# One PSUM bank moved from the side work to the exponentials, and the causal masks of the maxima added by TensorE: a causal attention in a four-block network

## The reference

```python
x = x + 0.5 * moe(layernorm(x));  x = x + attn0(layernorm(x));  x = x + 0.5 * moe(layernorm(x))
x = x + 0.5 * fp4(layernorm(x));  x = x + attn1(layernorm(x));  x = x + 0.5 * fp4(layernorm(x))

def attn0(x, Wqkv, Wout, bout):          # x: 4 sequences x 1024 tokens x 128; 16 heads of 8
    q, k, v = split_heads(x @ Wqkv.T)
    dots = einsum('bhid,bhjd->bhij', q, k) * 8 ** -0.5
    dots = where(key later than query, -inf, dots)
    return merge_heads(einsum('bhij,bhjd->bhid', softmax(dots), v)) @ Wout.T + bout
```

## Time and profile before

| | |
|---|---|
| median of 3 runs | 1891.05 us (1888.12 to 1892.08) |
| profiled execution, its own time | 1890.3 us |
| its span, first to last instruction | 1888.3 us |
| first exponential unit of the first attention | at 358.2 us |
| first exponential unit of its last round | at 870.1 us |
| mean granted TensorE clock | 0.929 |

### The profile page before, as it was taken

How to read it: one execution, slowest core, us unless ns; L and a number is a source line. 1 busy time by engine, 2 the same in 40 slices (tenths; PEclk the granted TensorE clock), 3 DMA queues, 4 the chain that set the end, 5 groups by cost and what they waited for, 6 DMA issues and landing times. The chain is left out here.

```text
span 1888.3 us, 35242 instructions
## 1 busy us (share of the span) xinstructions
PE 1582.2 (84%) x12162; PEld 1091.1 (58%) x12167; DVE 1220.6 (65%) x2516; ACT 1056.5 (56%) x2103; POOL 693.1 (37%) x1145
## 2 busy tenths in 40 slices
PE   6997975899999999999799799346788888988774
PEld 5666863555555555553666577234566766667653
DVE  6633558887887888883664366465656777766544
ACT  2433432488888888887243244213566667667651
POOL 0786552111111111111058665352234545544342
PEclk9998997899999999999699899767899999999987
DMA  6122322011111111110413123200000000000000
GB/s 246 38 78 66 109 68 70 23 40 29 27 36 29 34 29 28 40 29 12 183 45 88 59 82 101 102 1 1 2 2 2 5 5 8 5 8 8 7 4 12
DMA packets 50494, 83.08 MB, mean 44 GB/s; under 512 B 11124, under 2 KB 35124, under 8 KB 49652
## 3 DMA queue, kind: packets, MB, share of 16 engines
q1 hardware_dynamic: 41236, 62.07, 11.4%
q0 software_dynamic: 9088, 18.76, 2.9%
HBM read 43.18 MB, written 31.22 MB: 39 GB/s over the span
## 5 line engine op out<-in xcount | busy, mean ns | idle before, releaser
L1920 DVE TENSOR_REDUCE z_parts<-z_pM 128x4 f32<-128x512 f32 x576 | 373.0, 685 | 95.9 <-PE z_pM L1658 92.1
L1835 ACT ACTIVATE z_Pr<-z_pE 128x512 f32<-128x512 f32 x576 | 322.2, 596 | 86.7 <-PE z_pE L1682 83.9
L1682 PE MATMUL z_pE<-z_QM,z_QK 128*128 128x512 f32 x576 | 251.0, 438 | 8.9 <-DMA z_QM<-z_Q 6.6
L2027 POOL TENSOR_SCALAR_AFFINE_SELECT z_Pr<-z_Pr 128x512 f32<-128x512 f32 x128 | 81.3, 635 | 481.2 <-ACT z_Pr L1835 481.2
L1658 PE MATMUL z_pM<-z_KM,z_Q 128*128 128x512 f32 x576 | 233.4, 410 | 1.5 <-DVE z_Q L1910 0.9
L1682 PEld LDWEIGHTS z_pE<-z_QM,z_QK 128*128 128x128 f32 x576 | 108.1, 188 | 159.3 <-ACT z_Pr L1835 91.5
L356 POOL DMA_INDIRECT slot_results<-m_yq,m_xq x156 | 153.7, 985 | 108.5 <-ACT m_yq L561 79.9
L332 POOL DMA_INDIRECT slot_rows<-m_XN,m_dest x128 | 129.3, 1010 | 94.5 <-DVE m_dest L650 59.2
L1695 PE MATMUL z_pO<-z_Pr,z_V 128*9 128x512 f32 (+3 forms) x1536 | 159.3, 488 | 0.1
L974 PE MATMUL f_gup<-s_wguT,f_xT 128*128 128x352 f32 x234 | 102.6, 523 | 33.8 <-DVE f_src L1281 18.9
L1658 PEld LDWEIGHTS z_pM<-z_KM,z_Q 128*128 128x128 f32 x576 | 109.4, 191 | 18.4 <-DVE z_parts L1920 3.2
(11 more groups left out here) (290 smaller groups left out, 3870.3 us busy)
## 6 DMA issues: line engine op xcount, KB each, us to landing
slot_rows<-in_c_pad SPq DMA_DIRECT2D x2, 5070.0 KB, 24.6
m_xq<-slot_rows SPq DMA_DIRECT2D x38, 260.0 KB
z_QM<-z_Q SPq DMA_DIRECT2D x128, 64.0 KB, 2.0
z_KM<-z_QK SPq DMA_DIRECT2D x60, 128.0 KB, 2.4
m_raw<-in_gu SPq DMA_DIRECT2D x2, 2048.0 KB, 8.7
m_XN<-slot_results SPq DMA_DIRECT2D x8, 512.0 KB
m_raw<-slot_results SPq DMA_DIRECT2D x8, 512.0 KB, 5.6
slot_results<-m_yq,m_xq POOLq DMA_INDIRECT x156
```

What stands on the lines that cost most here:

```text
L1682: mm(pE[e % 2][:, :].rearrange("p (h c) -> p h c", h=4), QK[G % RING][:, kt * P:(kt + 1) * P], QM[half][:, :, q * P:(q + 1) * P], start=Tr ...
L1835: a.activation(Pr[j % 4][:, :, q * P:(q + 1) * P], pE[e % 2][:, :].rearrange("p (h c) -> p h c", h=4), ACT.Exp, scale=DH0 ** -0.5).then_in ...
L1920: v.tensor_reduce(parts[:, qt, kb, :], pM[n % 3][:, :].rearrange("p (h k) -> p h k", h=4), AX.X, ALU.max).then_inc(maxed, 1)
L2027: g_.affine_select(blk, blk, [[0, 4], [1, P]], ALU.is_ge, 0.0, base=0, channel_multiplier=-1).then_inc(selected, 1)
```

## The change

The side work gives one of its two banks to the exponentials. `pE` becomes three banks, and an exponential unit waits for unit e - 3 to be done instead of e - 2. All side work goes through the one bank `pX`, and the waits of each step are put on the last reader of the step before. The slots of the side work are set anew, and the order of the projections becomes first half of queries, first half of keys, second half of keys, second half of queries. The transfer of the keys waits for three projections of its round instead of two. ScalarE's mask writes and their semaphore go; every diagonal maximum unit is followed by the bf16 matmul that round 0 had.

```diff
-        pE = [s.ps(f"pE{u}", [P, 512]) for u in range(2)]
+        pE = [s.ps(f"pE{u}", [P, 512]) for u in range(3)]
-        pX, pO = [s.ps(f"pX{u}", [P, 512]) for u in range(2)], s.ps("pO", [P, 512])
+        pX, pO = s.ps("pX", [P, 512]), s.ps("pO", [P, 512])
...
-        AT_M1, AT_O1, AT_FIN, AT_K, AT_O0, AT_Q, AT_M0 = 4, 10, (13, 14), (16, 18), 21, (23, 29), 27
+        AT_M1, AT_O1, AT_FIN, AT_O0, AT_M0 = 4, 11, (14, 16), 22, 29
+        Q_LOW, K_LOW, K_HIGH, Q_HIGH = 2, 0, 1, 3
+        AT_PROJECT = (7, 18, 25, 31)
+        ORDER = (Q_LOW, K_LOW, K_HIGH, Q_HIGH)
...
-                        sp.wait_ge(split_done, 4 * (G + 2) + 2)
+                        sp.wait_ge(split_done, 4 * (G + 2) + 3)
                         sp.wait_ge(sm_ready, NM * (G + 1))
                         spread_keys(G + 2, slice(0, SEQ0), k_masked[G % 2])
...
-                    if G and kb == qt:
-                        pe.wait_ge(filled, len(DIAG) * (G - 1) + DIAG.index(n) + 1)
                     last = mm(pM[n % 3][:, :].rearrange("p (h k) -> p h k", h=4), Q[G % 2][:, qt * P:(qt + 1) * P],
-                              KM[G % 2][:, :, kb * P:(kb + 1) * P], start=(G == 0 or kb < qt), stop=(G > 0 or kb < qt), skip_group_check=True)
-                    if G == 0 and kb == qt:
+                              KM[G % 2][:, :, kb * P:(kb + 1) * P], start=True, stop=(kb < qt), skip_group_check=True)
+                    if kb == qt:
                         last = mm(pM[n % 3][:, :], identb[:, :], after_query[:, :], start=False, stop=True, skip_group_check=True)
...
-                    need(pe, exp_done, NE * G + e - 1)
-                    mm(pE[e % 2][:, :].rearrange("p (h c) -> p h c", h=4), QK[G % RING][:, kt * P:(kt + 1) * P],
+                    need(pe, exp_done, NE * G + e - 2)
+                    mm(pE[e % 3][:, :].rearrange("p (h c) -> p h c", h=4), QK[G % RING][:, kt * P:(kt + 1) * P],
...
                         if e == AT_M1:
+                            need(pe, split_done, min(4 * (G + 2), 4 * NG))
                             need(pe, m_kept, 2 * G + 1)
                             turn_maximum(G, 1)
+                        if e == AT_PROJECT[0] and further:
+                            need(pe, m_kept, 2 * G + 2)
+                            project(G + 2, Q_LOW)
                         if e == AT_O1 and G > 0:
-                            need(pe, split_done, min(4 * (G + 2), 4 * NG))
+                            need(pe, *((split_done, 4 * (G + 2) + 1) if further else (m_kept, 2 * G + 2)))
                             turn_output(G - 1, 1)
                         if e in AT_FIN and first:
-                            need(pe, m_kept, 2 * G + 2)
+                            need(pe, o_normed, 2 * G)
+                            need(pe, fin_kept, 2 * (G // 4 - 1) + AT_FIN.index(e))
                             turn_batch(G // 4 - 1, AT_FIN.index(e))
-                        if e in AT_K and further:
...
+                        if e == AT_PROJECT[1] and further:
+                            need(pe, split_done, 4 * (G + 2) + 1)
+                            need(pe, o_normed, 2 * G)
                             if first:
...
+                                need(pe, fin_kept, 2 * (G // 4))
+                            project(G + 2, K_LOW)
                         if e == AT_O0:
...
+                            if further:
+                                need(pe, split_done, 4 * (G + 2) + 2)
+                            else:
+                                need(pe, o_normed, 2 * G)
                             turn_output(G, 0)
-                        if e in AT_Q and further:
...
+                        if e == AT_PROJECT[2] and further:
+                            need(pe, o_normed, 2 * G + 1)
+                            project(G + 2, K_HIGH)
                         if e == AT_M0 and more:
-                            need(pe, o_normed, 2 * G + 1)
+                            if further:
+                                need(pe, split_done, 4 * (G + 2) + 3)
+                            else:
+                                need(pe, o_normed, 2 * G + 1)
                             turn_maximum(G + 1, 0)
+                        if e == AT_PROJECT[3] and further:
+                            need(pe, m_kept, 2 * G + 3)
+                            project(G + 2, Q_HIGH)
...
-                def fill_mask(G, n):
...
-                    act.wait_ge(maxed, NM * G + n - 2)
-                    a.activation(pM[n % 3][:, :], after_query[:, :], ACT.Copy).then_inc(filled, 1)
...
-                        if more and e + 2 in DIAG:
-                            fill_mask(G + 1, e + 2)
```

More of the change, by code:

```diff
@@ L1623, in project @@
                     for w, xx, a, b in ((wh, xh, True, False), (wh, xl, False, False), (wl, xh, False, True)):
-                        last = mm(pX[BANK[i]][:, :], w[:, c:c + P], xx[:, xs], start=a, stop=b)
+                        last = mm(bank(G, i)[:, :], w[:, c:c + P], xx[:, xs], start=a, stop=b)
                     last.then_inc(proj_done, 1)
@@ L1667, in turn_maximum @@
                     c = slice(half * 512, half * 512 + 512)
-                    mm(pX[0][:, :], identr[:, :], Q[G % 2][:, c], start=True, stop=False, skip_group_check=True)
+                    mm(pX[:, :], identr[:, :], Q[G % 2][:, c], start=True, stop=False, skip_group_check=True)
                     for j in range(4):
-                        last = mm(pX[0][:, j * P:(j + 1) * P], mw[:, 4 * half + j, :, :].rearrange("p h c -> p (h c)"), identr[:, :],
+                        last = mm(pX[:, j * P:(j + 1) * P], mw[:, 4 * half + j, :, :].rearrange("p h c -> p (h c)"), identr[:, :],
                                   start=False, stop=(j == 3), skip_group_check=True)
@@ L1701, in turn_output @@
                     for j in range(4):
-                        last = nc.tensor.transpose(pX[half][:, j * P:(j + 1) * P], oT[:, j * P:(j + 1) * P], ident[:, :])
+                        last = nc.tensor.transpose(pX[:, j * P:(j + 1) * P], oT[:, j * P:(j + 1) * P], ident[:, :])
                     last.then_inc(o_turned, 1)
@@ L1707, in turn_batch @@
                     for j in range(4):
-                        last = nc.tensor.transpose(pX[half][:, j * P:(j + 1) * P], at[:, half * 4 + j, :], ident[:, :])
+                        last = nc.tensor.transpose(pX[:, j * P:(j + 1) * P], at[:, half * 4 + j, :], ident[:, :])
                     last.then_inc(fin_turned, 1)
@@ L1910, in split @@
                     v.scalar_tensor_tensor(dst[:, (i % 2) * 512:(i % 2) * 512 + 512], high[:, :].bitcast(F32),
-                                           rows[:, 3 - i // 2:4 - i // 2], pX[BANK[i]][:, :], ALU.mult, ALU.add).then_inc(split_done, 1)
+                                           rows[:, 3 - i // 2:4 - i // 2], bank(G, i)[:, :], ALU.mult, ALU.add).then_inc(split_done, 1)
                 def max_unit(G, n):
@@ L1953, in main @@
                             output(G - 1, 1)
-                        for i in range(2):
-                            if n == AT_K[i] + LATE and further:
-                                split(G + 2, i, i)
+                        for k in range(4):
+                            if n == AT_PROJECT[k] + LATE and further:
+                                split(G + 2, ORDER[k], k)
                         if n == AT_O0 + 2:
                             output(G, 0)
-                        for i in range(2):
-                            if n == AT_Q[i] + LATE and further:
-                                split(G + 2, 2 + i, 2 + i)
                         if n < NM and more:
```

37 lines of the change are left out of this document (13 added, 24 removed).

## The result

The kernel after takes 1920.5 us (median of 4 runs, 1916.9 to 1924.67), beside 1889.59 for the kernel before: a ratio of 1.0168, 95% interval 1.0142 to 1.0194, some 31 us slower. The forecast of 1930 was right in direction and in order of size, 8 us too high in the loss. The profiled execution took 1916.9 with a span of 1915.0.

What follows compares the result with a forecast made beforehand. In full rounds TensorE was taken as a stream without holes except one 0.35 us wait. Terms 27.8 + 13.7 + 5.2 + 2.4 - 5.3 - 1.9 - 3.1 = +38.8 us on 1891.05 gave 1930, range 1907 to 1943.

Steps and rivals of the forecast that it cites:

- C: Maximum turn at slot 29 waits for VectorE's split: stall 0.37 us in 14 rounds, +5.2 us (0 to 8).
- E: Inserted masks and projection cover unit 10's wait for queries, 0.35 us in rounds 0 to 14: -5.3, late rounds -1.9.
- A: Diagonal masks moved to TensorE: 120 bf16 matmuls at 0.232 us, +27.8 us (25.8 to 36).
- The rival that TensorE had slack: Masks fall into TensorE's holes at no cost and relief stays: -10.3 us, 1880.8; chance 0.03.
- The sentence on the Trainium skill's 131 ns per matmul: 512-column matmuls in a stream at about 131 ns: masks would cost 15.7 us, forecast 12 us lower; not adopted.
- What ScalarE is spared is worth nothing: Full rounds: removing 120 mask writes, 72 us, from ScalarE buys nothing, since TensorE did not wait for it.
- B: Projection at slot 25 waits for VectorE to read the output turned at 22: 0.98 us in 14 rounds, +13.7.
- D: Rest of the shared bank: nothing from turn 29 to projection 31; batch turns in rounds 4, 8, 12, +2.4 us.
- F: Third exponential bank where ScalarE paces: -1.2 us in round 14, -1.5 in round 15, -0.4 at round 0's start.
- The rival of the free bank: Shared side bank costs no time, only masks count: +17.5 us, 1908.5; chance 0.10.
- The rival of late spreads: Query spreads come late at round starts, each of 14 rounds losing 1 us: +14, 1944; chance 0.08.

Runs made afterwards that it cites:

- masks only: Kernel before with only the diff's mask part, TensorE adding the diagonal masks: ratio to before 1.0124, stretch +19.0 us.
- the doubled masks: Kernel after with each mask matmul issued twice: ratio to the kernel before 1.0279, stretch +23.3 us against the kernel after.
- the later turns: Kernel after with output turn at slot 21, projections at 26 and 32, maximum turn at 31: ratio to before 1.0096, full rounds 35.18 us.
- banks and slots only: Kernel after with ScalarE's mask writes put back: ratio to the kernel before 1.0084, stretch +10.4 us.
- divide sooner: Kernel after with VectorE dividing the output turned at slot 22 before maximum unit 23 instead of 24: ratio to before 1.0127.
- the turn at 31 and ScalarE's masks: Kernel after with ScalarE's mask writes put back, output turn at 21, projections at 26 and 32, maximum turn at 31: ratio to before 0.9971.

## Why the prediction was right

The forecast for a full round was 36.55 by its own terms, and the trace has 36.37. The 0.18 between them are 0.07 in C and 0.105 in E.

**A, masks paid in full.** Right in the full rounds. 0.233 where I took 0.232, shown by the masks alone, by their doubling and by what is left when the stalls are taken out. The rival that TensorE had slack falls with them, although its weight loads are listed as busy for only 18.4 of 36.4 us. The sentence on the Trainium skill's 131 ns per matmul ("TensorE: Matmul & The Clock Gate", Back-to-back issue gap) is answered as well: no 512-column matmul of these rounds came under 0.21 behind its like. The isolated gap of the same section, 216 ns, is what the doubled masks show for bf16 behind bf16 (0.215); float32r behind float32r steps by 0.232.

**What ScalarE is spared is worth nothing.** Right in the full rounds, though the size of the relief was not: ScalarE's busy time fell by 54 us and not 72, since its listed durations overlap. In round 0 the relief was worth 1.8 us. Slots 0 to 4 took 6.99 us before and 5.44 with the masks on TensorE. ScalarE has a table load of 1.28 to do there, and before it wrote masks besides; that this is the reason was not tested by itself.

**B, the projection at 25.** Right, 0.97 for 0.98, and the cause is shown by moving the reader. The walk through VectorE's order gave 2.65 from turn to multiplication, and the trace has 2.65.

**C, the maximum turn at 29.** The cause was right, the size 0.30 for 0.37: -1.0 us. TensorE came to the turn 4.07 us after the projection's start and not 3.97 (641.90 + 0.23 - 638.06), VectorE ended its split after 4.22 and not 4.18.

**D, the rest.** The batch turns cost 1.7 instead of 2.4. Rounds 4, 8 and 12 are 1.62 longer than a usual one, with waits of 0.53 in slot 16 and 0.19 in slot 18 and none in slot 14; the kernel before already lost 0.17 in its slots 16 to 18, which the prediction left out. That leaves 0.55 three times. After the turn at 29, the projection at 31 cost nothing, as forecast.

**E, the wait for the queries.** Mis-sized. It was worth 0.455 a round, not 0.35: unit 10, having waited, also had its weight load uncovered, and the output turn behind it, in slot 10, took 0.105 more. I added that 0.16 of a wait where I made new stalls and forgot it where one went. That is some 1.5 us. Rounds with late spreads gave 3.0 and not 1.9; that is partly chance. The trace of the kernel after has no late spread, but masks only, banks and slots only and divide sooner still show some.

**F, where ScalarE paces.** Mis-sized most. Round 0 was forecast to grow by 2.45 and grew by 0.11; the lighter ScalarE gives 1.8 there and the third bank 0.6. The last round gave 2.4 instead of 1.5. And the term missed that in the new slots the third bank also carries the full rounds (0.41 in most of them); that did not harm the sum, because the bank is there.

In sum, rounded: round 0 -2.3, E -1.5 and -1.1, C -1.0, D -0.7, last round -0.9, and small ones, together -7.3 against the 38.8. The measured stretch is +31.5. The ones named here all err the same way, so the forecast was not brought close by errors that cancel.

The rival of the free bank, 1908.5, is not what happened but is nearly what the later turns made of it. The rival of late spreads did not occur in the kernel after. Unit 0 of a round waited for queries only with the turn at 31 and ScalarE's masks, 1.3 us in three rounds.

## What to carry to other kernels

When one engine's starts follow each other without a hole, price a change by that engine alone, and read this from start to start, not from its busy share: work moved onto it from an engine that was 84% busy cost its whole length. In round 0, where TensorE did wait for ScalarE, eight more masks cost 0.6 of their 1.7 us. A buffer shared by several steps costs what its last reader is late, and that reader is late by whatever stands before it in its own order; count those instructions one by one. And before taking out the one visible wait, look for the engine that stands just behind it: of 0.455 us taken away, 0.35 came back from ScalarE, until a further bank let it lag.

## What the runs showed of the hardware

A bf16 matmul of 512 columns takes 0.233 us of TensorE between float32r ones and 0.215 behind another of its kind, at a granted clock of 1.00. The matmul after it is listed as starting 0.03 to 0.04 later and lasting 0.58, so its own row can't be used to price it. ScalarE's exponentials and mask writes on 128x512 are listed for 0.60 and start 0.49 and 0.52 apart in the rows shown when they follow each other: 120 of them less took 54 us off its busy time. A wait that TensorE has to make costs more than its listed idle time: 0.97 us were lost where 0.71 was listed, and 0.38 where none was.
